# Both attentions of a four-stage kernel: how x is loaded, where memsets stand, and how the first strips are gathered

## What is computed

```python
# L0, the "ratio" attention: 16 heads of 16 columns
dot = jnp.einsum('bhid,bhjd->bhij', q, k)
vals = q_norm_sq + k_norm_sq.transpose(0, 1, 3, 2)
scores = dot * dot / (vals - 2.0 * dot + EPSILON)
scores = scores + mask                # -1e9 above the diagonal
out = jnp.einsum('bhij,bhjd->bhid', softmax(scores), v)
...
# L1, the "zeroed" attention: one 16x48 weight for all heads
qkv = jnp.einsum('bhce,ef->bhcf', xh, Wqkv) + bqkv
att = jnp.einsum('bhqe,bhke->bhqk', q, k) / jnp.sqrt(jnp.float32(he))
att = jax.nn.softmax(att * mask, axis=-1)   # mask: zeros, not -inf
out = jnp.einsum('bhqk,bhke->bhqe', att, v)
...
x = x + _L0_attn_ref(_layernorm(x, axis=-1), ...)
x = x + _L0_ffn_ref(_layernorm(x, axis=-1), ...)     # low rank, gelu
x = x + _L1_attn_ref(_layernorm(x, axis=-1), ...)
x = x + _L1_ffn_ref(_layernorm(x, axis=-1), ...)     # ternary weights
```

## Time and profile before

| | value |
|---|---|
| median of 3 runs | 3171.81 us (3169.41 to 3182.85) |
| the profiled execution, its own time | 3176.6 us |
| its span in the profile | 3174.6 us |
| TensorE busy, weight loads | 2825.4 us (89%), 1976.1 us (62%) |
| VectorE, ScalarE, GpSimd busy | 74%, 64%, 55% |
| mean granted clock of TensorE | 0.958 |

### The profile page before, as it was taken

How to read it: one execution, slowest core, us unless ns; L and a number is a source line. 1 busy time by engine, 2 the same in 40 slices (tenths; PEclk the granted TensorE clock), 3 DMA queues, 4 the chain that set the end, 5 groups by cost and what they waited for, 6 DMA issues and landing times. The chain is left out here.

```text
span 3174.6 us, 76595 instructions
## 1 busy us (share of the span) xinstructions
PE 2825.4 (89%) x28516; PEld 1976.1 (62%) x28516; DVE 2363.9 (74%) x6131; ACT 2039.8 (64%) x3686; POOL 1747.2 (55%) x3054
## 2 busy tenths in 40 slices
PE   2899999999999999988997788888888888789998
PEld 1677677777667777642332566666666666556666
DVE  2899899998889989855233566766666666489998
ACT  1888888888888888842332355555555555467776
POOL 1666666666666666634110355555555655466665
PEclk8999999999999999987998799999999999999999
DMA  5333333333333333310000645443544444000001
GB/s 159 64 64 64 64 63 64 63 61 59 57 57 61 63 59 64 64 40 5 1 0 1 112 70 89 71 86 70 84 77 77 79 76 87 7 8 21 27 21 34
DMA packets 109266, 181.96 MB, mean 57 GB/s; under 512 B 26336, under 2 KB 95712, under 8 KB 96416
## 3 DMA queue, kind: packets, MB, share of 16 engines
q1 hardware_dynamic: 105440, 176.28, 30.5%
q10 hardware_dynamic: 3456, 0.79, 0.2%
HBM read 115.92 MB, written 60.29 MB: 56 GB/s over the span
## 5 line engine op out<-in xcount | busy, mean ns | idle before, releaser
L789 POOL TENSOR_TENSOR ratio_scores<-ratio_scores,ratio_max_cols 128x512 f32<-128x512 f32 (+3 forms) x1024 | 725.7, 724 | 374.0 <-DVE ratio_max_cols L699 369.9
L1273 DVE TENSOR_REDUCE zeroed_max_cols<-bank 128x1 f32<-128x512 f32 (+3 forms) x1024 | 445.7, 480 | 192.4 <-PE bank L185 190.8
L182 PE MATMUL bank<-ratio_k_stack,ratio_q_stack 102*128 102x512 bf16 (+7 forms) x2048 | 510.9, 305 | 81.8 <-DMA ratio_k_stack<-ratio_norms_k 46.7
L1166 ACT ACTIVATE zeroed_prob<-bank 128x512 f32<-128x512 f32 x640 | 376.8, 593 | 300.3 <-PE bank L1056 206.2
L699 DVE CUSTOM_DVE_ANT_0 ratio_scores<-bank,ratio_scores 128x512 f32<-128x512 f32 (+3 forms) x1024 | 472.4, 489 | 22.1
L689 DVE TENSOR_TENSOR ratio_scores<-bank,ratio_inverse 128x512 f32<-128x512 f32 x640 | 436.3, 682 | 57.0 <-PE bank L182 42.3
L561 ACT ACTIVATE ratio_prob<-bank 128x512 f32<-128x512 f32 x640 | 378.3, 592 | 124.0 <-PE bank L475 123.0
L472 PE MATMUL bank<-const_f_sb,ratio_scores 128*128 128x128 f32 x2560 | 413.0, 275 | 3.0 <-ACT ratio_prob L561 2.5
L550 ACT ACTIVATE ratio_inverse<-bank 128x512 f32<-128x512 f32 x640 | 381.7, 597 | 51.2 <-PE bank L185 50.9
L1385 POOL TENSOR_SCALAR_AFFINE_SELECT zeroed_prob<-zeroed_prob 128x256 f32<-128x256 f32 (+1 forms) x640 | 228.1, 365 | 333.2 <-ACT zeroed_prob L1166 331.5
L185 PE MATMUL bank<-const_b_sb 128*128 128x128 bf16 x2048 | 391.9, 223 | 1.7 <-issue 1.7
(11 more groups left out here) (169 smaller groups left out, 5612.0 us busy)
## 6 DMA issues: line engine op xcount, KB each, us to landing
ratio_q_stack<-ratio_parts_q SPq DMA_DIRECT2D x192, 128.0 KB
ratio_k_stack<-ratio_parts_k SPq DMA_DIRECT2D x192, 128.0 KB
zeroed_q_stack<-zeroed_parts_q SPq DMA_DIRECT2D x192, 128.0 KB, 4.4
zeroed_k_stack<-zeroed_parts_k SPq DMA_DIRECT2D x192, 128.0 KB, 7.6
ratio_parts_q<-ratio_parts SPq DMA_DIRECT2D x96, 128.0 KB
ratio_parts_k<-ratio_parts SPq DMA_DIRECT2D x96, 128.0 KB
zeroed_parts_q<-zeroed_parts SPq DMA_DIRECT2D x96, 128.0 KB
zeroed_parts_k<-zeroed_parts SPq DMA_DIRECT2D x96, 128.0 KB
```

The source lines that it names most:

```text
L182: i = e.matmul(bank[:, off:off + w], qs[0:rows, s, hh, ib * P:(ib + 1) * P], ks[0:rows, s, hh, 0:w], start=(k == 0), stop=mask is None, sk ...
L789: i = e.tensor_tensor(seg, seg, mx[:, pair % M_BUFS, c:c + 1].to_broadcast([P, w]), ALU.subtract)
L1166: e.activation(prob[:, n % FOLD_PROBS, 0:wd], exp_banks[n % 2][:, 0:wd], ACT.Exp, scale=0.25).then_inc(s["prob"])
L1273: i = e.tensor_reduce(mx[:, pair % FOLDS, c:c + 1], bank[:, off:off + (ib + 1) * P], AX_X, ALU.max)
```

## The change

- `load_start` issues only rows 0 and 1 of x. Row b+2 is issued by SP in the ratio attention, ahead of what it does for the half 2b+1.
- The memsets of the rows of ones on DVE stand later: in the ratio attention behind the two normalisations of row 0, in the zeroed attention behind the values of half 0.
- Half 0 of both attentions is gathered in two sets: the strips of the first 4 heads with a semaphore of their own (`gathered_first`), then those of the other 4 (`gathered0`). Units 0 to 9 need the first set, units from 10 on the second. In the ratio attention the norms of half 0 are sent ahead of all strips.
- From half 1 on, the norms are sent between the strips of q and those of k (before: behind both).
- `PREP_AT`: q, k and the norms of the next half are prepared at slots 2, 4 and 6 (before: 3, 5 and 7); `root` moves from slot 2 to 3.
- In the zeroed attention, q and k of half 1 are prepared from within the loop, at slots 2 and 5 of half 0 (`Z_SECOND_AT`), not ahead of it.

```diff
@@ load_start
             weights.load(q)
-            for b in range(1, net.B):
-                e.dma_start(net.xb(b), row(b)).then_inc(net.x_loaded[b], 16)
+            e.dma_start(net.xb(1), row(1)).then_inc(net.x_loaded[1], 16)
...
-PREP_AT = ({3: "q", 5: "k", 7: "n", 9: "va", 12: "vb", 16: "x0"}, {0: "x1", 3: "q", 5: "k", 7: "n", 9: "va", 13: "vb"})
-R_ROOT_AT, R_XN_AT, R_STATS_AT = 2, (14, 18), (15, 17)
+PREP_AT = ({2: "q", 4: "k", 6: "n", 9: "va", 12: "vb", 16: "x0"}, {0: "x1", 2: "q", 4: "k", 6: "n", 9: "va", 13: "vb"})
+R_ROOT_AT, R_XN_AT, R_STATS_AT = 3, (14, 18), (15, 17)
...
@@ ratio_attention, pe
             def denoms(n):
-                q.wait_ge(*gathered(n // HALF_UNITS))
+                q.wait_ge(s["gathered_first"], 16 * 14)
+                if n >= N_UNITS:
+                    q.wait_ge(*gathered(n // HALF_UNITS))
...
@@ ratio_attention, dve
             stats(0, 0)
             stats(0, 1)
-            e.memset(ones(qs), TWO_ONES).then_inc(s["q_ones"])
             normal(0, 0)
             normal(0, 1)
+            e.memset(ones(qs), TWO_ONES).then_inc(s["q_ones"])
             split(0, 0)
...
@@ ratio_attention, sp
-            for half in range(halves):
+            first, second, all_heads = slice(0, GROUP), slice(GROUP, HALF), slice(0, HALF)
+            send_parts(0, 0)
+            send_parts(0, 1)
+            send_norms(0, 0)
+            send_norms(0, 1)
+            gather_parts(0, 0, first, s["gathered_first"])
+            gather_parts(0, 1, first, s["gathered_first"])
+            gather_norms(0, s["gathered_first"])
+            gather_parts(0, 0, second, s["gathered0"])
+            gather_parts(0, 1, second, s["gathered0"])
+            for half in range(1, halves):
+                b, m = divmod(half, 2)
+                if m and b + 2 < B:
+                    e.dma_start(net.xb(b + 2), x_dram[b + 2].rearrange("(t p) d -> p t d", p=P)).then_inc(net.x_loaded[b + 2], 16)
+                sem = gathered(half)[0]
                 send_parts(half, 0)
                 send_parts(half, 1)
-                gather_parts(half, 0)
-                gather_parts(half, 1)
+                gather_parts(half, 0, all_heads, sem)
                 send_norms(half, 0)
                 send_norms(half, 1)
-                gather_norms(half)
+                gather_parts(half, 1, all_heads, sem)
+                gather_norms(half, sem)
...
@@ zeroed_attention, pe
+                if half == 0 and at in Z_SECOND_AT:
+                    project(1, Z_SECOND_AT.index(at))
...
-            for half in range(2):
-                project(half, 0)
-                project(half, 1)
+            project(0, 0)
+            project(0, 1)
             values(0, 0)
             values(0, 1)
...
@@ zeroed_attention, dve
-            e.memset(ks[STACK:P, :, :, :].rearrange("p s h t -> p (s h t)").bitcast(F32), TWO_ONES).then_inc(s["k_ones"])
...
             values(0, 0)
             values(0, 1)
+            e.memset(ks[STACK:P, :, :, :].rearrange("p s h t -> p (s h t)").bitcast(F32), TWO_ONES).then_inc(s["k_ones"])
...
@@ zeroed_attention, sp
-            for half in range(2):
+            send_parts(0, 0)
+            send_parts(0, 1)
+            gather(0, slice(0, GROUP), s["gathered_first"])
+            gather(0, slice(GROUP, HALF), s["gathered0"])
+            for half in range(1, halves):
                 send_parts(half, 0)
                 send_parts(half, 1)
-                gather(half)
...
+                gather(half, slice(0, HALF), gathered(half)[0])
```

More of the change, by code:

```diff
@@ L898 @@
 GROUPS_FROM, ROW_STEPS = ZEROED_LAG + ATTEND_LAG + 6, (67, 70, 72, 77)
+Z_SECOND_AT = (2, 5)
 BIAS_FROM = 57
@@ L1200, in prepare @@
                         keep_x(half // 2 + 1, Z_TURN_AT.index(at))
+                if half == 0 and at in Z_SECOND_AT:
+                    split(1, Z_SECOND_AT.index(at))
                 if half + 2 < halves and at in Z_SPLIT_AT:
@@ L1209, in act @@
             keep_x(0, 1)
-            for half in range(2):
-                split(half, 0)
-                split(half, 1)
+            split(0, 0)
+            split(0, 1)
             keep_suffix(0)
```

48 lines of the change are left out of this document (22 added, 26 removed).

## The result

The changed kernel took 3091.32 us, the median of four runs (3088.38 to 3099.67), against 3171.11 us before: the ratio is 0.9737, 95% interval 0.9714 to 0.976. It is 80 us faster. The forecast was 3121.0 us, 50.8 us faster, with a range down to 3100.

The account below looks back on a forecast made before the run. Three nearly full engines in fixed order bound the ratio attention, so only stalls can be won; 19 + 3.5 + 4.3 + 25 - 4 + 3 = 50.8 us gave 3121.0 us, 80% range 3100 to 3143 us.

Parts of the forecast that it names:

- Part 1: Start of the kernel: two rows of x instead of sixteen let the block start at 7.9 us; gain 19 us, bounds 16–20.
- Part 2: Ratio attention's start: DVE's memset moves behind the normalisation, into its wait for the squares; gain 3.5 us.
- Part 3: Ratio attention's first gathering: norms sent first, half-size strips; first product earlier by 4.3 us, bounds 0.7 and 7.6.
- the 0.72 us a strip: Assumed time per half strip in the first gatherings, against 1.04 us for a whole strip of 128 KB.
- Part 4: Ratio attention's half boundaries: earlier preparation and norms ahead of k's strips end PE's slot 17 wait; 25 us, bounds 12–33.
- Part 5: Ratio attention's preparation at slots 2, 4, 6: q waits longer for squares; loss 4 us, bounds gain 20, loss 33.
- Part 6: Zeroed attention: first product 8.8 us earlier, mostly lost to a wait at dots(20); gain 3 us, bounds -5 and 9.
- Half strips cost like whole ones: Rival on both attentions' first gatherings: halving strips saves no transfer time; 7.6 us less gain, 3129 us, chance 0.13.
- The boundary comes back elsewhere: Rival: DVE waits for ScalarE in slots 2 to 6 instead of slot 17; 3142 us, chance 0.15.
- Slower: Rival: DVE waits out ScalarE's pair exponential at all three preparations, 98 us a run; 3215 us, chance 0.03.
- The new slots help: Rival: root out of q's way gains 1.2 us per even half, boundaries won whole; 3091 us, chance 0.1.
- What would show it: Forecast trace signs at the start, first products, norms' and squares' waits, including a 4 us zeroed-attention wait.

Follow-up runs that it names:

- x alone: Kernel before with one edit: two rows of x loaded at the start, the others in the ratio attention; 3154.96 us, ratio 0.9942.
- the new order of the norms and the old slots: Changed kernel with q, k, norms back at slots 3, 5, 7 and root at 2; 3101.01 us, ratio 0.9771.
- The norms' order alone: Kernel before with one edit: in every half the norms are sent between the strips of q and those of k; 3125.68 us, ratio 0.985.

## Why the prediction was wrong, step by step

- **Part 1, x as needed (19 us).** Measured 20.6 us: the block starts at 6.97 us, not at 7.9, and nothing became late. The engines did not start worse without the rest. "Cost 0" for the moved loads held in the changed kernel, and in the kernel before with x alone. With the new order of the norms and the old slots they cost 6.5 us. The reason given, that they delay no strip, looked at the place in SP's queue alone: a gathering of norms issued right behind strips and ahead of the load landed 1.0 us later.
- **Part 2, the memset (3.5 us).** Measured 2.5 us. The memset's 3.47 us are hidden, but the first two instructions of the normalisation now take 2.10 us together instead of 0.73 (9.52 us in the timeline above), while GpSimd fills its own rows until 11.5 us. That the two go together is argued from the timeline only.
- **Part 3, the first gathering (4.3 us, bounds 0.7 and 7.6).** Measured 7.1 us: from the end of the first normalisations to the product 34.5 us before, 27.5 after. The step that failed is the 0.72 us a strip, half way between the bounds. Near enough, the half strips take the time of their issue, 2.63 us for six, and 2.6 us behind the last: from the first strip's issue to the product it took 8.4 us, where the whole strips took 17.0. In the zeroed attention twelve half strips of 64 KB need 7.5 us from issue to product (1656.26 to 1663.76), where twelve of 128 KB needed 14.17. So half the bytes took half the time, and the rival did not hold. The Trainium skill (DMA: Bandwidth & Descriptors, Measured) calls transfers under 64 KB dominated by descriptors; the half strips are of 64 KB and not under it, so the rival read more into the rule than it says, and these runs do not test it.
- **Part 4, the boundary (25 us, bounds 12 and 33).** This is the step that failed and put the time outside the range. The wait goes in all halves, as said. But the size was cut to 25 because three engines are nearly full, and capped at PE's 33.0 us. The norms' order alone shortened the stage by 47.5 us. Both the cut and the cap were wrong: a half was longer by the whole wait and 0.16 us more, and behind six of the long ones the clock was halved for 3.4 us, 1.5 us each, which no row of waits shows and which I had not looked for, though the granted clock of before has it.
- **Part 5, the slots (-4 us, bounds -33 and 20).** The sign was wrong. From 1279.0 us (old slots, norms' order) to 1274.5 us the slots gain some 4 us, with x hidden besides. The waits for the squares rose (56.0 against 47.1 us), so the longer wait that I saw is there, but it lengthens no half; and PE's wait for a bank that DVE reads, 23.0 us in 61 pieces with the old slots, is 9.3 us in 19 with the new, and this I did not look at. Halves of even number went from 41.97 to 41.69 us, in each of the seven profiles with the new slots, which makes 15 x 0.28 = 4.2 us. Root, on which I had put the possible gain, gives about 7 us in the kernel before and leaves these halves at 41.96 us.
- **Part 6, the zeroed attention (3 us, bounds -5 and 9).** Inside the bounds: some 5 us by the stages of all profiles, -2.3 in the pair of the table. The mechanism was right: a wait of 2.24 us at `dots(20)` (about 4 forecast), most of the gain returned. The first product came 12.9 us earlier and not 8.8: 6.7 us by the strips (3.6 forecast) and 6.2 ahead of them (5.2).
- **The rivals.** "Half strips cost like whole ones" fell with 7.1 us. "The boundary comes back elsewhere" fell: the wait for squares grew by 2.1 us and not by 30. "Slower" did not occur. "The new slots help" had the number, of which its first half (18 us by root) is not found, and its second (the boundary whole) is, only larger. The measured 3091 us is no point for it: its 18 us by root are missing and its boundary is 14.5 us too small.
- **What would show it.** First statistics at 6.97 us (8 forecast), first score product at 39.10 us (42.5), no wait for norms at slot 17 (right), squares 56.0 us (54), zeroed first product 28.5 us (31).

With the measured sizes the sum would have been 20.6 + 2.5 + 7.1 + 47.5 + 4 + 5 = 87 us, or 82 with nothing for part 6. The spans differ by 79 us when the 7.5 of the low-rank network are taken off, and the medians by 80 (76 to 91 by the interval of the ratio).

## What to carry to other kernels

When all engines of a tight loop stop for one transfer, count its wait whole, look at the granted clock right behind it, and do not take the sum of one engine's named waits for the most that can be won. A small transfer that is waited for is late first by what was issued just ahead of it on its queue (2.2 us against 4.7 here), and only then by what stands right behind it (1.0 us more, and nothing where the queue was empty). And work moved into a loop to start the loop earlier has to be paid there: if the other engines wait at that point anyhow, it is cheaper ahead of the loop.

## What the runs showed of the hardware

- TensorE's granted clock went to half for 3.4 us behind six of eleven waits of 1.9 to 2.75 us in a loop that was else 94% busy, and this cost about 1.5 us each time. In the nine kernels and repeats whose longest wait for the norms in the loop was 0.8 us or less there is no such stretch up to 1300 us.
- A gathering of 24 KB landed 2.2 us after its issue when the strips before it had landed, with or without 512 KB issued 0.3 us behind it (2.25 and 2.23 us). Issued right behind six strips of 128 KB it took 4.5 to 4.7 us, and 5.6 us with the 512 KB behind it as well.
- Twelve transfers of 64 KB on one queue took 7.5 us from the first issue to the matmul that waited for them, twelve of 128 KB 14.2 us.
- SP needs 0.40 us to issue a row of x (512 KB) when it stands alone, and 1.44 us each when 15 stand in a row.
- One kernel, in two executions, had a low-rank network of 321.6 or 329.2 us, with the clock at half for 38 or 65 us at its start.
